# Four steps a turn for VectorE in the joint stage, its local rows by loads of their own, and the sort's bonds ahead of its rows

## What is computed

```
# layer 0, means over the edges of each node, both ways
a_in  = seg_mean((x @ W_in.T  + b_in)[src],  dst)
a_out = seg_mean((x @ W_out.T + b_out)[dst], src)
x = layernorm(x + gru(concat(a_in, a_out), x))
# layer 1, one message per edge, summed over src
m = relu(concat(x[src], x[dst], bond) @ W1 + b1) @ W2 + b2
x = layernorm(x + x + segment_sum(m * sigmoid(bond @ Wa + ba), src))
```

## Time and profile before

| what | us |
|---|---|
| the profiled execution / its span | 13790.1 / 13788.4 |
| GpSimd (POOL) busy, whole span | 9705.6 (70%) |
| TensorE (PE) busy | 8650.6 (63%) |
| VectorE (DVE) busy | 8351.6 (61%) |
| ScalarE (ACT) busy | 2713.3 (20%) |
| the sort: first to last scatter issued | 2369.1 to 6651.3 |
| the joint stage: first to last gather issued | 6675.7 to 8783.5 |

### The profile page before, as it was taken

One profiled execution on the slowest core, in us unless ns is written; L12 is line 12 of the kernel. 1 busy time (PEld: TensorE's weight loads), 2 busy tenths in 40 slices (PEclk: granted clock), 3 DMA queues, 4 the chain that ended last, 5 costly groups with the idle time before them and its releaser, 6 DMA issues. The chain is left out here.

```text
span 13788.4 us, 248865 instructions
## 1 busy us (share of the span) xinstructions
PE 8650.6 (63%) x53687; PEld 7661.1 (56%) x53688; DVE 8351.6 (61%) x29389; ACT 2713.3 (20%) x7251; POOL 9705.6 (70%) x10125
## 2 busy tenths in 40 slices
PE   3777776333333333333577777797888888888876
PEld 2555554333333333333577777556777777777775
DVE  6555555666666666666677777554444455444444
ACT  0000000111111111111000000154444444444444
POOL 3777776777777777777777777306777777777774
PEclk9555555555656555666788888898999999999998
DMA  5822223666666666666677777513333334333336
GB/s 178 308 54 54 54 54 84 197 198 196 199 196 199 197 199 196 199 196 199 174 187 186 186 186 186 95 52 76 80 79 79 80 88 94 80 79 80 79 79 82
DMA packets 2665496, 1884.08 MB, mean 137 GB/s; under 512 B 1375795, under 2 KB 2460371, under 8 KB 2664784
## 3 DMA queue, kind: packets, MB, share of 16 engines
q1 hardware_dynamic: 1505269, 806.75, 22.1%
q0 software_dynamic: 377360, 782.89, 19.9%
q10 hardware_dynamic: 782662, 292.60, 8.8%
HBM read 1509.53 MB, written 483.44 MB: 145 GB/s over the span
## 5 line engine op out<-in xcount | busy, mean ns | idle before, releaser
L1846 POOL DMA_INDIRECT p<-q_rows,small x3432 | 3250.1, 947 | 1643.5 <-issue 1000.0
L1051 PE MATMUL bank<-p,ring 128*128 x6656 | 1549.0, 426 | 2714.7 <-DVE ring L972 2711.5
L1051 PEld LDWEIGHTS bank<-p,ring 128*128 128x128 f32 x6656 | 1437.8, 328 | 2826.1 <-issue 2826.1
L1110 POOL DMA_INDIRECT edges_a<-ring,small x1664 | 1635.7, 983 | 563.1 <-issue 441.4
L1110 POOL DMA_INDIRECT edges_b<-ring,small x1664 | 1632.5, 981 | 507.6 <-issue 441.1
L799 POOL DMA_INDIRECT ring<-in_x,ring x1664 | 1573.9, 946 | 533.7 <-issue 530.0
L1884 PE MATMUL bank<-ring 128*128 128x256 f32 x3432 | 1205.4, 437 | 766.4 <-DVE p L1796 766.1
L830 PE MATMUL bank<-ring 128*128 128x129 f32 x3328 | 1240.3, 491 | 617.8 <-DMA ring<-in_x,ring 525.1
L1252 POOL DMA_INDIRECT ring<-in_x,small x1352 | 1278.7, 946 | 463.2 <-issue 411.3
L1272 PE MATMUL bank<-p,ring 128*128 128x129 f32 x8360 | 1194.3, 312 | 525.1 <-DVE ring L1200 525.1
L1272 PEld LDWEIGHTS bank<-p,ring 128*128 128x128 f32 x8360 | 1157.7, 226 | 562.5 <-issue 562.5
(11 more groups left out here) (289 smaller groups left out, 14195.4 us busy)
## 6 DMA issues: line engine op xcount, KB each, us to landing
p<-rows_by_slot SPq DMA_DIRECT2D x418, 928.0 KB
p<-edges_b SPq DMA_DIRECT2D x530, 262.0 KB
p<-edges_a SPq DMA_DIRECT2D x520, 262.0 KB
bonds_by_dst<-in_bond ACTq DMA_DIRECT2D x5, 20625.0 KB, 159.1
ring<-edges_a ACTq DMA_DIRECT2D x1792, 33.0 KB
p<-q_rows,small POOLq DMA_INDIRECT x3432
ring<-edges_b ACTq DMA_DIRECT2D x1664, 33.0 KB
ring<-bonds_by_dst ACTq DMA_DIRECT2D x1672, 32.0 KB
```

The lines of the kernel that those rows point to most:

```text
L1051: last = nc.tensor.matmul(found[q][:, j, :], hot_t[g % GRPS][:, QUAD * h + j, :], x, start=True, stop=True, skip_group_check=True)
L1110: pool.indirect_dma_start(out=c.edges[s], out_offset=bass.IndirectOffsetOnAxis(ap=pos[:, k:k + 1], axis=0), in_=rec[:, k, :], in_offset=No ...
L1846: pool.indirect_dma_start(out=gath[g][:, k, :], out_offset=None, in_=c.q_dram, in_offset=bass.IndirectOffsetOnAxis(ap=gidx[g][:, k:k + 1], ...
```

## The change

In the joint stage VectorE's loop has four steps a turn (`TURN_V` = 4) and 52 turns instead of 26. Local rows are no longer loaded with the gather ids, but by a DMA of their own (`load_locals`, 32 bytes for each partition) into one of four buffers, with semaphores `s_loc` of their own. SP issues it at the end of its step u, for step u+4, behind a wait for `prepare_in(u)`, which reads the buffer that is overwritten. The ids load is 32 bytes for each partition. In the sort SP's step u loads bonds first and rows second.

```diff
 # sort_records, SP
                         u = i * LOOK + g
+                        sp.wait_ge(s_sc[2 * (g % GRPS)], i * (2 * QUAD * 16) + g // GRPS * (QUAD * 16))
+                        load_bonds(u, 2 * (g % GRPS))
                         sp.wait_ge(s_hot, u * 4 + 12)
                         load_rows(u + 2, g % 2)
-                        sp.wait_ge(s_sc[2 * (g % GRPS)], i * (2 * QUAD * 16) + g // GRPS * (QUAD * 16))
-                        load_bonds(u, 2 * (g % GRPS))
 # sum_rest
+    TURN_V, s_loc = 4, c.sems("s_locals_in", 4)
-    ids = [... 2 * HALF words ... for n in range(LOOK)]
+    ids = [c.small[:, 128 + n * HALF:128 + (n + 1) * HALF] for n in range(LOOK)]
+    local = [c.small[:, 256 + n * HALF:256 + (n + 1) * HALF] for n in range(TURN_V)]
 # sum_rest, SP
+            def load_locals(u, n):
+                sp.dma_start(local[n], c.slots_d[:, bass.ds(u + B_GROUP, 1), LOCAL * HALF:(LOCAL + 1) * HALF]
+                             .rearrange("p o w -> p (o w)")).then_inc(s_loc[n], 16)
             for g in range(AHEAD):
                 load_ids(g, g)
+            for n in range(TURN_V):
+                load_locals(n, n)
...
                         load_windows(u, g % 2, edges)
                         sp.wait_ge(s_agg_in, u * NI + (IN_0 - (LOOK - AHEAD - 1) * NI))
                         load_ids(u + AHEAD, (g + AHEAD) % LOOK)
+                        sp.wait_ge(s_hot_in, u + 1)
+                        load_locals(u + TURN_V, g % TURN_V)
 # sum_rest, VectorE
-                dve.wait_ge(s_ids[g], 16 * i + (16 * ahead + 16))
+                dve.wait_ge(s_loc[g], 16 * i + (16 * ahead + 16))
-            with dve.Fori(0, QSTEPS // LOOK) as i:
-                step.loop(i, LOOK * NO)
-                for g in range(LOOK):
+            with dve.Fori(0, QSTEPS // TURN_V) as i:
+                step.loop(i, TURN_V * NO)
+                for g in range(TURN_V):
```

More of the change, by code:

```diff
@@ L1141, in sum_rest @@
     lo_out = c.small[:, 24:24 + QPS * QW]
-    ids = [c.small[:, 128 + n * 2 * HALF:128 + (n + 1) * 2 * HALF].rearrange("p (f k) -> p f k", k=HALF) for n in range(LOOK)]
+    ids = [c.small[:, 128 + n * HALF:128 + (n + 1) * HALF] for n in range(LOOK)]
+    local = [c.small[:, 256 + n * HALF:256 + (n + 1) * HALF] for n in range(TURN_V)]
     out_bank = [c.bank[0:2], c.bank[2:4]]
@@ L1148, in load_ids @@
             def load_ids(u, g):
-                sp.dma_start(ids[g].rearrange("p f k -> p (f k)"),
-                             c.slots_d[:, bass.ds(u + B_GROUP, 1), GATHER * HALF:(LOCAL + 1) * HALF]
+                sp.dma_start(ids[g], c.slots_d[:, bass.ds(u + B_GROUP, 1), GATHER * HALF:(GATHER + 1) * HALF]
                              .rearrange("p o w -> p (o w)")).then_inc(s_ids[g], 16)
+            def load_locals(u, n):
+                sp.dma_start(local[n], c.slots_d[:, bass.ds(u + B_GROUP, 1), LOCAL * HALF:(LOCAL + 1) * HALF]
+                             .rearrange("p o w -> p (o w)")).then_inc(s_loc[n], 16)
             def load_windows(u, g, edges):
@@ L1174, in _ @@
                 sp.wait_ge(s_ids[g], 16 * (QSTEPS // LOOK + (1 if g < AHEAD else 0)))
+            for n in range(TURN_V):
+                sp.wait_ge(s_loc[n], 16 * (QSTEPS // TURN_V + 1))
         @block.vector
@@ L1186, in prepare_in @@
                 a, b = g % 2 * HALF, (g % 2 + 1) * HALF
-                dve.wait_ge(s_ids[g], 16 * i + (16 * ahead + 16))
-                nc.vector.tensor_tensor(hot_in[:, a:b, :], ids[g][:, 1, :].unsqueeze(2).to_broadcast([P, HALF, P]),
+                dve.wait_ge(s_loc[g], 16 * i + (16 * ahead + 16))
+                nc.vector.tensor_tensor(hot_in[:, a:b, :], local[g].unsqueeze(2).to_broadcast([P, HALF, P]),
                                         c.iota_p.unsqueeze(1).to_broadcast([P, HALF, P]), ALU.is_equal).then_inc(s_hot_in, 1)
@@ L1194, in prepare_out @@
                 lo = lo_out[:, a * QW:b * QW]
-                dve.wait_ge(s_win[2 * (g % 2) + h], i * (8 * LOOK * (b - a)) + 16 * (b - a) * (LOOK // 2 * ahead + g // 2 + 1))
+                dve.wait_ge(s_win[2 * (g % 2) + h], i * (8 * TURN_V * (b - a)) + 16 * (b - a) * (TURN_V // 2 * ahead + g // 2 + 1))
                 step.link(nc.vector.tensor_tensor(
                     lo.rearrange("p (j k) -> p j k", k=QW), win[:, first + a:first + b, :, 0],
-                    c.blk_s[:, bass.ds(i * (LOOK * QPS) + ((g + LOOK * ahead) * QPS + a), b - a)]
+                    c.blk_s[:, bass.ds(i * (TURN_V * QPS) + ((g + TURN_V * ahead) * QPS + a), b - a)]
                     .unsqueeze(2).to_broadcast([P, b - a, QW]), ALU.subtract))
@@ L1226, in _ @@
                 prepare_in(0, g)
-            with dve.Fori(0, QSTEPS // LOOK) as i:
-                step.loop(i, LOOK * NO)
-                for g in range(LOOK):
-                    u, g2, ahead = i * LOOK + g, (g + 2) % LOOK, (g + 2) // LOOK
+            with dve.Fori(0, QSTEPS // TURN_V) as i:
+                step.loop(i, TURN_V * NO)
+                for g in range(TURN_V):
+                    u, g2, ahead = i * TURN_V + g, (g + 2) % TURN_V, (g + 2) // TURN_V
                     blocks = slot_values(c, mybir.EngineType.DVE, S_BLOCKS, u * MIX, HALF + QPS)
@@ L1236, in _ @@
                     prepare_in(i, g2, ahead)
-            step.end(QSTEPS // LOOK)
+            step.end(QSTEPS // TURN_V)
             dve.wait_ge(s_acc_in, HS + ADDED_IN_0)
@@ L1253, in _ @@
                                 out=gath[at][:, 0:D], out_offset=None, in_=c.ins["x"],
-                                in_offset=bass.IndirectOffsetOnAxis(ap=ids[g][:, 0, k:k + 1].bitcast(I32), axis=0),
+                                in_offset=bass.IndirectOffsetOnAxis(ap=ids[g][:, k:k + 1].bitcast(I32), axis=0),
                             ).then_inc(s_g[at], 16)
```

## The result

The changed kernel takes 14194.88 us (median of 4 runs, 14190.77 to 14201.54), the kernel before 13777.87 in the same comparison: the ratio is 1.0303, 95% interval 1.0285 to 1.0321. It is slower by 417 us. Forecast were 14300 and a range of 14060 to 14530.

A forecast was written before the change was run, and what follows sets the result against it. VectorE was taken to set the joint stage's end, GpSimd right behind, and GpSimd to bound the sort. Joint stage +527 and sort -10 on 13790.1 gave 14307, so 14300 for the median; range 14060 to 14530.

The forecast's parts named there:

- The new wait on SP and the ring: Joint stage: windows wait for `prepare_in`, closing a circle of SP, DMA and VectorE; 12.6 us a round against 10.1.
- The tail: Last seven joint-stage steps, empty slots gathering one row: slow transfers count in full, +60 us, between +40 and +130.
- The shorter turn: VectorE's joint-stage loop: half-length turn stays loaded, removing 96.4 us of idle time, but worth nothing once SP's wait binds.
- Its worth alone: Joint stage with only VectorE's four-step turn: between 0 and -75 us, taken as -48, GpSimd bounding at 10.0 a step.
- The sort: Sort's start: bonds sent at once let the first scatter start at about 2359.4, -9.7 us; steady part 0.
- The sum: Whole kernel: 13790.1 + 527 - 10 = 14307 us for the profiled execution, 14300 for the median.
- The weighing of the landing: Windows' DMA: trace's 2.05 us from issue to traffic preferred to the skill page's 0.6; page's round 1.4 us shorter.
- The rival that counted on slack: Joint stage: SP's new wait is already passed or hidden by the windows' slack, giving 13722 us; chance 0.07.

The follow-up runs named there:

- e1: Changed kernel, but SP loads locals of step u+1 under the old wait for `sum_in(u-3)`, without the wait for `prepare_in(u)`: 13758.08 us, ratio 0.9991 to the kernel before.
- e7: Changed kernel, but SP waits for the second half of `prepare_out(u)` instead of `prepare_in(u)`, then loads locals of step u+3: 14028.67 us.
- e8: e1 with the gather ids of the last six, empty steps taken from 16 steps before: 13717.55 us, again 13719.16 us.
- e2: Kernel before, eight-step turn kept, with locals by their own DMA behind the ids and the new wait for `prepare_in(u)` between: 14214.29 us.
- e9: e8 with VectorE's turn of eight steps, ids and locals loaded together in eight buffers each: 13742.79 us, ratio 0.9965 to the kernel before.
- e3: Kernel before with only the sort's edit, bonds ahead of rows: 13761.81 us, ratio 0.9990.
- e6: e2 without its wait, so the kernel before with locals by a DMA of their own behind the ids: 13775.18 us, ratio 1.0000.
- e4: Changed kernel, but SP waits for the first half of `prepare_out(u)` instead of `prepare_in(u)`, then loads locals of step u+3: 13789.77 us.

## Why the prediction was right, by its steps

- **The new wait on SP and the ring: right.** Counted out of the trace as 12.6 us a round, measured 12.29 (12.32 with the wait alone). The terms, averaged over steps 6 to 193 of the changed kernel's trace:

| term | forecast | measured |
|---|---|---|
| end of `prepare_in` to the first window: SP's wake, locals, register load | 2.02 | 1.90 |
| first window issued to the second half of `prepare_out` | 8.1 | 7.83 |
| second half, up to `prepare_in` | 1.3 | 1.34 |
| `prepare_in` | 1.22 | 1.22 |
| sum | 12.6 | 12.28 |

So nearly all of the 0.3 lies in the landing and in SP's part. I had let the landing of all five windows (8.1) set the second term. Its 7.83 are 5.91 to the start of the first half, when three windows have landed, and 1.92 for that half: the other two made VectorE wait over 0.1 us more in only 11 of 188 rounds. And in one round of four the register load takes some 0.52 and not 1.07 us. 208 rounds of 0.32 make 66 us of the 99 by which the stage was forecast too long; the end makes the rest.

- **The tail: right in place, too dear.** The last 13 rounds took 182.9 us; at 12.29 they would have been 160. So the end costs 23, and I had taken 60, from a stage that ran at 10.1. The slower the round, the less the end adds: over 13 steady rounds it adds 64 us in e1 (9.99), 36 in e7 (11.35), 23 here. The likely reason is that in the ring the DMA engines had more room (0.59 busy against 0.71) before the slow gathers came; no run separates that. The steps with one row for all are six (202 to 207, as e8 shows), not seven.
- **The shorter turn: worth nothing once the ring binds, right** (e2 against the change: the two ratios' intervals overlap, and the stages differ by 12 us). **Its worth alone was mis-sized:** -48 was taken for the stage with the wait free; e1 has -13.5 and -10.9. The pace came out as reckoned, 10.0 on GpSimd, but the slow end swallowed 20 of the 33 us. The step that failed is that I took the end's cost as staying, less the one long fetch. Whoever comes there at a faster pace waits there longer: with one-row gathers the last 13 rounds take 174 to 194 us at rounds of 9.99 to 12.32, with other rows 129 to 131. Even without the slow end the stage gains 28 to 32 and not 48 (e8 against e9).
- **The sort: -7.0 where -9.7 was forecast.** I let `pos` set the first scatter, but it is still the bonds. They leave only at 2350.73, as SP issues three tables ahead of them, and land 5.3 us later.
- **The sum.** Stage +427.7, sort -7.0, together +420.7; the two spans differ by 406.2. The other 14.5 lie where no effect of an edit shows: the start of the sort is 4.5 us sooner, the scatters from first to last 6.6 shorter, what follows the joint stage 3.7. SP's order did change under the scatters, but their time with and without that edit overlaps (e3). The kernel before's profiled execution was one of its slower ones (13790.1 against a median of 13777.87), and e2 and e6, without the edit in the sort, have much of the same: 3.5 to 3.8 us shorter scatters and 2.6 to 6.2 less behind the stage.
- **The weighing of the landing.** The 2.05 us from issue to traffic were read from whole microseconds, and are too long: in the changed kernel's trace the first packet of a window starts 1.34 us behind the first issue (median of its rounds; 1.31 at the least). What the round needs is the landing itself, and there the row held (7.83 where 8.1 was taken). The Trainium skill (DMA: Bandwidth & Descriptors, Specifications) gives about 0.6 us to the first byte on this path; the trace has twice that, so it disagrees, but by 0.7 us and not by the 1.4 that I took. With the page's figure the prediction's round would have been 11.2, an estimate; measured is 12.29.
- **The rival that counted on slack** fell as its conditions said. It needed a round under 10, and e4 shows that with one it would have been right: a wait of the same kind, 2.5 us earlier in VectorE's step, and the loss is gone but for 0.06 us a round.

## What to carry to other kernels

A wait that a queue's engine makes for a consumer is not judged by whether it "has long been met", nor by how many buffers there are, but by what stands behind it in program order: here a load that was meant to run four steps ahead held up another, which the same consumer needs next. Walk from the new wait round to itself, add up latencies, and compare the sum with the step of the engine that bounds; under it the wait is nearly free (e4), over it the excess is paid in every round (e7, the change), and what is saved elsewhere is worth next to nothing (e2 against the change). If an older wait in the same program already implies that the buffer is free (here `sum_in(u-3)`), use it, and load less far ahead.

## What was not expected of the hardware

- Indirect gathers whose 128 indices are all the same row are slow: DMA share 0.95 at 66 GB/s, against 0.71 at 178 with different rows, in the same stretch of the same stage, and 0.74 us a packet against 0.14. Six steps of them cost 63 us in the kernel that reaches them at full pace.
- VectorE's turn of eight steps fetches 5 blocks of 8 KB on each turn and stops for about 3 us; with the turn of four steps the fetches are gone (2 in 1000 us, of all engines, instead of 63).
